# Reordering TensorE, ScalarE and the load queue inside the group loop of a two-layer graph network on Trainium2

## What is computed

```
h  = relu(layernorm(x))
xp = h @ W                               # 4 heads of 32
e  = leaky_relu(a_s[src] + a_d[dst])     # self loops are added
m  = segment_max(e, dst);  w = exp(e - m[dst])
x  = x + relu(segment_sum(w * xp[src]) / segment_sum(w) + bias)
h  = relu(layernorm(x))
agg   = segment_sum(edge_attr @ We + be, dst)
comb  = concat(h, agg)
neigh = segment_sum(comb[src], dst)
x  = x + relu((comb + neigh) @ W1 + b1) @ W2 + b2
```

## Time and profile before

| what | value |
|---|---|
| median of 3 runs | 3248.04 us (3247.97 to 3249.55) |
| the profiled execution, its own time | 3249.53 us |
| its span, first to last instruction | 3247.6 us |
| PE, DVE, POOL, ACT busy | 66%, 57%, 47%, 34% of the span |
| mean granted TensorE clock | 0.772 of full |
| group loop | from about 130 to 2930 us |

### The profile page before, as it was taken

The page is one execution under the profiler, slowest core; times in us unless marked ns, Lnnn a source line. Parts: engine busy times, 40 slices in busy tenths (PEclk is TensorE's granted clock), DMA queues, the critical chain, the costliest instruction groups (busy, mean ns, idle before and its releaser), DMA issues.

```text
span 3247.6 us, 60418 instructions
## 1 busy us (share of the span) xinstructions
PE 2133.8 (66%) x16302; PEld 1640.0 (50%) x16302; DVE 1838.2 (57%) x6265; ACT 1095.0 (34%) x2343; POOL 1516.2 (47%) x1625
## 2 busy tenths in 40 slices
PE   4466665665666666656666676666676676667987
PEld 3354554554554545545445454454454445455766
DVE  7365666666666666656556565555555556564221
ACT  3333333333333344333333333333333233332000
POOL 3555555555555555554545555445444444550000
PEclk8666766766767766778878788788888788878999
DMA  9845545555555555565555655556555555655665
GB/s 195 121 137 163 167 139 163 155 153 162 155 153 163 148 165 172 152 182 150 179 153 174 173 170 180 149 162 177 159 153 176 166 147 172 180 138 189 209 198 159
DMA packets 395176, 532.44 MB, mean 164 GB/s; under 512 B 115603, under 2 KB 346723, under 8 KB 383665
## 3 DMA queue, kind: packets, MB, share of 16 engines
q1 hardware_dynamic: 344939, 415.35, 42.4%
q0 software_dynamic: 50112, 115.56, 15.9%
HBM read 385.48 MB, written 145.24 MB: 163 GB/s over the span
## 4 chain that ended last, share of the span: by engine, by line
PE 26%; DVE 21%; another core or an unknown queue 21%; issue 13%; DMA 8%; ACT 5%; SPq 5%; ACTq 1%; DVEq 1%
PE pv L1352 9%; PE pv L1284 5%; PE pt L1275 4%; ACT xsb L942 4%; DVE tabb L1640 4%; DMA state<-zpart 4%; DMA state<-sums 3%; PE pt L1253 2%; DVE big L1932 2%; PE pv L1409 2%; DVE lks L1915 1%; DVE fy L1759 1%; DVE fy L1768 1%; PE pt L1409 1%
## 5 line engine op out<-in xcount | busy, mean ns | idle before, releaser
L906 POOL DMA_INDIRECT big<-table,idx x1566 | 1489.2, 951 | 1372.4 <-issue 399.2
L942 ACT ACTIVATE xsb<-pt 128x343 f32 x1042 | 482.0, 463 | 1547.7 <-remote 922.0
L1253 PE MATMUL pt<-tabb 128*128 128x343 bf16 x1042 | 379.5, 364 | 448.1 <-ACT xsb L942 405.8
L1284 PE MATMUL pv<-big 128*128 128x128 f32 x3132 | 511.3, 329 | 8.0 <-issue 5.6
L1284 PEld LDWEIGHTS pv<-big 128*128 128x128 f32 x3132 | 476.3, 239 | 32.2 <-issue 13.7
L1352 PE MATMUL pv<-big 128*128 128x133 f32 x3132 | 391.6, 280 | 22.2 <-DVE big L1932 22.2
L1253 PEld LDWEIGHTS pt<-tabb 128*128 128x128 bf16 x1042 | 107.9, 104 | 553.8 <-ACT xsb L942 439.9
L1352 PEld LDWEIGHTS pv<-big 128*128 128x128 f32 x3132 | 367.9, 190 | 35.5 <-DVE big L1932 22.4
L1640 DVE TENSOR_TENSOR tabb<-pc,keyp 128x2064 bf16<-128x2064 bf16 x261 | 319.0, 1222 | 0.0
L942 ACT ACTIVATE xsb<-pa 128x343 f32 x521 | 240.9, 462 | 61.8
L1932 DVE TENSOR_TENSOR big<-big,pm 128x768 f32<-128x768 f32 x261 | 233.4, 950 | 30.8 <-ACT pm L942 19.0
(11 more groups left out here) (339 smaller groups left out, 3282.5 us busy)
## 6 DMA issues: line engine op xcount, KB each, us to landing
adj<-xsb SPq DMA_DIRECT2D x87, 1176.0 KB
big<-in_edge_attr_dram SPq DMA_DIRECT2D x87, 1152.0 KB
selb<-rel SPq DMA_DIRECT2D x87, 576.0 KB
pro<-adj SPq DMA_DIRECT2D x28, 896.0 KB
big<-table,idx POOLq DMA_INDIRECT x1566
state<-sums SPq DMA_DIRECT2D x87, 130.5 KB
sums<-state SPq DMA_DIRECT2D x87, 130.5 KB
pro<-adj SPq DMA_DIRECT2D x12, 672.0 KB
```

Source lines behind the costliest of these rows:

```text
L906: pool.indirect_dma_start(out=V[b][:, j, 0:rows], out_offset=None, in_=table, in_offset=bass.IndirectOffsetOnAxis(ap=index[b][:, j:j + 1], ...
L942: return nc.scalar.activation(out_, in_, func, **kw).then_inc(s(name), 1)
L1253: ins = nc.tensor.matmul(to, ohl[:, c, :], ohk[:, c, 0:KW], start=True, stop=alone)
L1284: ins = nc.tensor.matmul(sumA[b], SEL[b][:, j, :], AT[b][:, j, :], start=(j == 0), stop=(j == J - 1))
```

## The change

- PE's order becomes: projection of n-2, tails out, carries back, chunks 9 to 14 of n-1, peaks, chunks 15 to 17 of n-1, attribute sums 0 to 5 (in items with a job: none), the whole job, look-up, chunks 0 to 2 of n, the other attribute sums, chunks 3 to 5, transposition, chunks 6 to 8, weighted sum. Chunks 9 to 14 no longer stand behind the weighted sum, nor the projection inside it.
- ACT copies the selection ahead of the late chunks of n-1 (now 9 to 17), and chunks 0 to 2 only behind the fold and the normalisation.
- SP issues the load of the state, and the store of the residual, ahead of the attribute rows and so ahead of the wait for `vm_b`.
- POOL's stops move from gathers 11 and 14 to 9 and 12.
- DVE rescales the state behind the scan of the tails, and keeps the job's result behind the second set of edge marks.
- The projection of n-2 is waited for by `tailT_b`; the last two by a semaphore of their own.

```diff
-FILL = (10, 14)
-PAUSES = ((11, "mg_b"), (14, "look"))
+PAUSES = ((9, "mg_b"), (12, "look"))
+LEAD = (6, 0)
...
                 load_job(n, like)
-                if ahead is not None:
-                    load_attributes(n + 2, b, ahead)
                 if before_first:
                     sp.wait_ge(s("tab_out"), 32 * (TAB_CHUNKS + 1))
                 load_sums(n, base)
                 if not before_first:
                     store_residual(n - 1, base_before)
+                if ahead is not None:
+                    load_attributes(n + 2, b, ahead)
...
                 a(thruT[:, :], thruP, ACT.Copy, "thru_c")
-                if finish_before:
-                    keep_adjacency(n - 1, 1 - b, 15, 18)
                 after(act, s("sel_b"), n)
                 if not (isinstance(n, int) and n < 2):
                     act.wait_ge(s("vm_b"), n - 1)
                 a(SEL[b], selH, ACT.Copy, "selc_b")
-                if not is_extra:
-                    after_dma(act, s("adj_out"), n - 1)
-                    keep_adjacency(n, b, 0, 3)
-                else:
+                if finish_before:
+                    keep_adjacency(n - 1, 1 - b, 9, 18)
+                if is_extra:
...
                 if not is_extra:
-                    keep_adjacency(n, b, 3, 6)
+                    after_dma(act, s("adj_out"), n - 1)
+                    keep_adjacency(n, b, 0, 3)
...
                 if not is_extra:
-                    keep_adjacency(n, b, 6, 15)
+                    keep_adjacency(n, b, 3, 9)
...
-                job(n, like, 0, FILL[0])
+                if finish_before and not (isinstance(n, int) and n < 2):
+                    project_window(n - 2)
                 after(pe, s("pre1_b"), n)
                 after(pe, s("thru_c"), n)
                 nc.tensor.transpose(tailT, pre1[:, :, J - 1], ident[:, :]).then_inc(s("tailT_b"), 1)
-                job(n, like, FILL[0], FILL[1])
                 after(pe, s("tails_b"), n)
...
                 if finish_before:
-                    adjacency(n - 1, 15, 18)
+                    adjacency(n - 1, 9, 15)
...
-                job(n, like, FILL[1], NB)
                 after(pe, s("pkl_b"), n)
...
                 ins.then_inc(s("mg_b"), 1)
-                if not is_extra:
-                    adjacency(n, 0, 3, like)
+                if finish_before:
+                    adjacency(n - 1, 15, 18)
...
                 after(pe, s("merged"), n, 2)
-                attribute_sums(0, 3)
+                lead = LEAD[1 if parts_of(like) else 0]
+                attribute_sums(0, lead)
+                job(n, like)
...
                 ins.then_inc(s("look"), 1)
                 if not is_extra:
+                    adjacency(n, 0, 3, like)
+                attribute_sums(lead, J)
+                if not is_extra:
                     adjacency(n, 3, 6)
-                attribute_sums(3, J)
...
                 for q in range(QN):
-                    if q == QN - 1 and finish_before:
-                        project_window(n - 1)
...
                 ins.then_inc(s("vm_b"), 1)
-                if not is_extra:
-                    adjacency(n, 9, 15)
             stage(pe, item)
-            adjacency(NG - 1, 15, 18)
+            project_window(NG - 2)
+            adjacency(NG - 1, 9, 18)
...
                 select(n, b, extra_group)
-                if m is not None:
-                    rescale_state(m, 1 - b)
...
                     .then_inc(s("tails_b"), 1)
                 if m is not None:
+                    rescale_state(m, 1 - b)
                     add_sums(m, 1 - b)
...
-                keep_job(n, like)
                 after(dve, s("mg_b"), n)
...
                 if not is_extra:
                     edge_marks(n, 1)
+                    keep_job(n, like)
```

More of the change, by code:

```diff
@@ L1079, in _ @@
             stage(act, item)
-            keep_adjacency(NG - 1, 0, 15, 18)
+            keep_adjacency(NG - 1, 0, 9, 18)
             normalise_window(NG - 1)
@@ L1238, in project_window @@
                 ins = nc.tensor.matmul(finY, fhT[:, C:2 * C], wew[:, :], start=False, stop=True)
-                if isinstance(m, int) and m == NG - 1:
+                if isinstance(m, int) and m >= NG - 2:
                     ins.then_inc(s("ym_f"), 1)
@@ L1260, in adjacency, with job @@
                         ins.then_inc(s("ab_mm"), 1)
-            def job(n, like, lo, hi):
+            def job(n, like):
                 total = HP * parts_of(like)
-                hi = min(hi, total)
-                if lo >= hi:
+                if not total:
                     return
[L1268 to L1273, removed]
+                if isinstance(n, int):
+                    pe.wait_ge(s("ys2"), parts_of(like))
+                pe.wait_ge(s("aw_in"), n * 16 + (16 - JOB0 * 16))
+                pe.wait_ge(s("ab_ev"), n * J - (J - 15))
+                for i in range(total):
                     q, h = divmod(i, HP)
@@ L1276, in job @@
                                            stop=(i == total - 1))
-                if hi == total:
-                    ins.then_inc(s("jb_mm"), 1)
+                ins.then_inc(s("jb_mm"), 1)
             def item(n, b, it, like=0, is_extra=False):
@@ L1283, in attribute_sums @@
                     for j in range(lo, hi):
-                        ins = nc.tensor.matmul(sumA[b], SEL[b][:, j, :], AT[b][:, j, :],
-                                               start=(j == 0), stop=(j == J - 1))
-                    return ins
+                        nc.tensor.matmul(sumA[b], SEL[b][:, j, :], AT[b][:, j, :],
+                                         start=(j == 0), stop=(j == J - 1))
                 if is_extra or (isinstance(n, int) and n == 0):
@@ L1775, in finish_projection @@
             def finish_projection(m):
-                if isinstance(m, int) and m == NG - 1:
-                    dve.wait_ge(s("ym_f"), 1)
+                if isinstance(m, int) and m >= NG - 2:
+                    dve.wait_ge(s("ym_f"), m - (NG - 3))
                 else:
-                    dve.wait_ge(s("vm_b"), m + 2)
+                    after(dve, s("tailT_b"), m + 2)
                 dve.wait_ge(s("y_out"), m * 16 + 16)
```

## The result

The changed kernel takes 3659.48 us (median of 4 runs, 3656.16 to 3661.94) against 3248.8 us (3247.97 to 3258.16) for the kernel before: ratio 1.126, 95% interval 1.125 to 1.128. I had forecast 2990 us. Its profiled execution has a span of 3660.0 us for 3247.6, a mean TensorE clock of 0.743 for 0.772, and PE busy 60% for 66%.

A forecast was written before the change was run, and what follows sets the result against it. It took the pace to be set by POOL's gathers plus waits for PE's news, held until bursts end. 40 items x 3.0 us + 45 job items x 3.1 - 2 for the tail = 258 us saved: 2990 us, own range 2940 to 3060.

The forecast's parts named there:

- The first stop: POOL's stop at gather 9: held news of the peaks comes at t = 13.0; costs 2.6 us net, not 2.63.
- the second: POOL's stop at gather 12, for the look-up's news: read at about t = 18.1, costs 1.4 us net, as before.
- The carries: Behind the earlier scan and 0.45 us of rescaling: carries at t = 3.7, peaks ready at 6.6 instead of 10.2.
- Behind the look-up: Look-up's end to weighted sum's end: 10.6 us for 11.5 without a job; POOL's net wait 4.1 becomes 1.2.
- A second step: Look-up's end, 1.94 us after the peaks' news to its reading as before: t = 15.6 without a job; 19.1 with one.
- Rival 3: Chunks 12 to 17 ahead of peaks and job make PE wait for ACT's copies: slower, 3287 us; chance 0.15.
- Rival 2: Last burst of six gathers holds news of weighting and sum: 2 or 1.2 us more an item, 3124 us; chance 0.20.
- Rival 1: The peaks' news isn't held at t = 8, so the first stop costs nothing: 2919 us; chance 0.18.
- the rule that I set against the sum: PE's waits bring half rate behind the look-up: 2.8 us an item if a quarter did; left out of the forecast.
- The tail: Projection of n = 85 and chunks 9 to 14 of the last group ahead of its transposition: +2 us.

The follow-up runs named there:

- e1: The kernel before with only POOL's stops moved, from gathers 11 and 14 to 9 and 12: 3207.71 us, ratio 0.981.
- e8: The changed kernel with the store of the projection moved ahead of the attribute load: 3672.55 us, ratio 1.130 to the kernel before.
- e14: The changed kernel with a third GpSimd stop, ahead of gather 15 until the transposition's news is there: 3439.06 us, ratio 1.059 to the kernel before.
- e3: The changed kernel with chunks 6 to 8 moved from ahead of the weighted sum to ahead of its third part: 3485.02 us, 1.066 to the kernel before.
- e5: The changed kernel with chunks 6 to 8 inside the weighted sum and a third stop ahead of gather 15: 3096.42 us, 0.954 to the kernel before.
- e9: The changed kernel with the third stop ahead of gather 15, on the chip that holds no news: 3143.06 us, 1.196 to the kernel before there.

## Why the prediction was wrong

**What held.** The bound was read rightly: the news of TensorE is held by a burst of gathers (e1, e8, e14), and an early state load alone brings nothing (0.998). The load order and the rescaling cost nothing. GpSimd's times down to its last gather came within 0.1 us, in part by luck. The first stop began 0.3 us late and the news then came 1.7 us after the last gather's end, not 2.1, so its net wait was 2.2 us for 2.6. At the second, the look-up's news was read at 18.1 as forecast, but not because it was held: the look-up ended only at 17.4, behind the burst, and was read 0.7 us later. The carries were at 6.0 us from gather 0, not 3.7: L1774 stood 4 us for the store of the last projection, which SP issues behind the wait for `vm_b`. I had missed that step, and where news is held it was worth at most 0.5% (0.949 against 0.954, on two chips).

**The step that failed: "Behind the look-up".** I took 11.5 us from before, less three attribute sums and the projection, plus three chunks: 10.6. Measured: 1132.71 to 1148.54, 15.8. With a job I had 6.6 + 4.5 = 11.1; measured 2426.21 to 2445.64, 19.4. The term counted what TensorE does, and not what its chunks wait for. The change put ScalarE's copies of 3 to 5 behind fhT, and so made the copies, the chunks 6 to 8, and the whole weighted sum wait for the transposition's news. In item 29 that is 3.9 us of idling, 1.0 more for chunks paced by copies (1.50 us for 0.5) and 2.2 more for the sum, most of it by the low clock (6.4 us; 4.9 before, of which I had taken off 0.7 for the projection), less about 2 that the attribute sums and six chunks ahead of the transposition gave back at full clock: about 5. The diff shows all of it; I followed that handshake for the chunks ahead of the peaks and for these I didn't.

The stretch over whole traces, look-up's end to the weighted sum's end (median in us; items 3 to 37 have no job, items 57 to 82 one of 28 matmuls):

| kernel | no job | job |
|---|---|---|
| forecast | 10.6 | 11.1 |
| before | 11.5 | 10.5 |
| changed | 15.9 | 19.4 |
| chunks inside the sum (e3, A) | 15.4 | 14.7 |
| third stop (e14, D) | 16.0 | 14.3 |
| both (e5, B) | 11.0 | 10.7 |
| third stop where no news is held (e9, C) | 14.6 | 14.6 |

In the last row only the chunks' place is at work: some 4 us.

**A second step, smaller.** The look-up ends at 17.4 us from gather 0 for 15.6 forecast, and at 20.7 for 19.1 with a job. I had it 1.94 us behind the peaks' news, as before. But chunk 17 now stands between them and waits for the copy of chunk 15 (two before it, not three as for the others), and behind it come six attribute sums at the low clock. None of the repairs touches this in items without a job (17.4 in e5 too), and it is about what separates e5's 29.3 us an item from the 27.7 forecast.

**The rivals.** Rival 3 (the chunks' handshake holds TensorE) was the right mechanism in the wrong place and too small. Its own place did cost, though not by chunk 14, whose news came 0.2 us after its end, but by chunk 16, whose news came 3.3 us late, with that of the peaks: TensorE waits 3.84 us for the copies ahead of chunk 17. In item 63 the job starts at 14.0 us for 9.8 forecast, but its 28 matmuls took 6.3 us, not 8.7, and the look-up ended at 20.7 for 19.1. Rival 2 (the last burst holds, and the clock falls) is the other half; I priced it at 2 and 1.2 us, on the news of the weighting and the sum's parts, not on that of the transposition, and the third stop alone is worth 5 us in an item with a job. Either cause alone makes a loss: with the chunks moved and the news still held, 1.066; with the stop added and the chunks left, 1.059; with both cured, 0.954 (on three chips, each against its own kernel before). Together the two cures are worth 0.174, their separate gains sum to 0.131. I gave the two separate chances and never a joint price. Rival 1's condition is refuted where news is held and holds on C; its gain isn't seen there, since the changed kernel with the third stop lost 20%.

**The clock.** By the rule that I set against the sum, 2.8 us an item would be lost if a quarter of the stretch ran at half rate. 0.50 was granted for the chunks and the first 3.2 us of the sum, and the sum took 1.9 us more in item 29 and 1.8 in item 63 than the 4.5 that I had for its 36 records. The Trainium skill (TensorE: Matmul & The Clock Gate, HAM oscillation) says that waits put the array back to half rate and each streak starts cold; the trace agrees (0.98 while idle, then 0.50), and this belonged in the sum, as soon as an idle stretch stood ahead of fp32 matmuls.

**The tail** behind item 85's look-up was 10 us longer, not 2. Which of its steps makes this wasn't followed.

## What to carry to other kernels

When a chunk, copy or store is moved, follow the handshake it is part of through every engine's own order, both ways: the copy that frees a bank now stands behind whatever its engine does first, and the matmul that needs the bank stands ahead of whatever TensorE does next. If a signal reads late, let its producer finish earlier (the lateness grows if it is held) and let the suspected holder stand still at that point (it goes). And time a reordering on more than one chip before trusting its sign.

## What was not expected of the hardware

News of TensorE is held during bursts of indirect DMAs on four chips and not on the fifth, with the same program: peaks that end in a burst are heard 3.8 us later in item 29 of the changed kernel (7.9 in e8), and 0.35 us later on C. The kernel before takes 3247 to 3270 us on the four and 2628 on C, and its mean granted clock there is 0.85 to 0.86 for 0.77 to 0.79. One kernel with a trace on both kinds is the old order with three stops, 2618 us on C and 3150 on D: a gather takes 953 and 950 ns in them, a chunk's copy 463 in both, so the work isn't slower, the waits are longer and the granted clock lower. That the 19% of the kernel before lie in late news too is inferred: it has no trace on C. What in the gathers holds the news stays open; their issuing and their traffic stop together, and TensorE's ends are modelled, so the traces don't tell whether its results or only its signals come late. Open, too, are why one chip is free of it, and the changed kernel's own time on C, which wasn't measured; with the third stop it lost 20%.

Nor is all news in a burst held, or held to its end. In item 29 of the changed kernel ScalarE copies chunk 9 at 1117.03, 0.2 us after the end of chunk 11, with seven gathers still to come before the stop; the news of chunk 16, given in the same burst, comes 3.3 us late; and the transposition is heard 1.7 us late with two gathers more to come. The peaks were held to the stop in both that item and e8, and heard 1.5 to 1.7 us after the last gather's end (1127.42 to 1128.88 in e8, 1126.56 to 1128.27 in item 29). What makes one case and the other isn't settled, and I draw no rule.
